# Graph attention kernel: rows sorted in interleaved groups of 512, with one-hot matmuls in place of list and output scatters

## The reference

```python
# layer 0
scores = where(adj != 0, -arange(N), -inf); vals, idx = top_k(scores, 25)
agg = max over k of x[idx[k]]            # 0 joins the maximum where degree <= 25
x = layernorm(x + relu(concat([x, agg]) @ W0 + b0))
# layer 1
Wh = x @ W1; e = leaky(s1[i] + s2[j] + emb[adj]); alpha = softmax(where(adj, e, -1e9))
x = layernorm(x + elu(layernorm(alpha @ Wh) * gamma + beta))
```

## Time and profile before

| what | us |
|---|---|
| median of 3 runs | 3402.12 (3399.23 to 3404.91) |
| span of the profiled execution, first to last instruction | 3411.3 |
| POOL busy | 2503.8 (73%) |
| DVE busy | 2400.8 (70%) |
| PE busy | 1642.6 (48%) |
| ACT busy | 1115.1 (33%) |

### The profile page before, as it was taken

How to read it: one execution, slowest core, us unless ns; L and a number is a source line. 1 busy time by engine, 2 the same in 40 slices (tenths; PEclk the granted TensorE clock), 3 DMA queues, 4 the chain that set the end, 5 groups by cost and what they waited for, 6 DMA issues and landing times.

```text
span 3411.3 us, 25793 instructions
## 1 busy us (share of the span) xinstructions
PE 1642.6 (48%) x5249; PEld 1185.4 (35%) x5259; DVE 2400.8 (70%) x5775; ACT 1115.1 (33%) x2307; POOL 2503.8 (73%) x2619
## 2 busy tenths in 40 slices
PE   8046456443463435643555345544555434466454
PEld 1034334332342323432333233333433323344343
DVE  7798877567775677767695778767785465566666
ACT  3124343323333234332343334232232212223234
POOL 3576777777677776777777777777777777777775
PEclk9976667666666666666677666676676666677776
DMA  7667876655566556675666666555544444444332
GB/s 259 211 202 258 287 240 198 226 171 183 187 197 227 171 184 198 199 246 162 216 216 194 214 195 215 163 182 153 165 131 115 123 113 116 118 118 117 106 106 72
DMA packets 221587, 610.02 MB, mean 179 GB/s; under 512 B 68849, under 2 KB 112882, under 8 KB 194802
## 3 DMA queue, kind: packets, MB, share of 16 engines
q0 software_dynamic: 122880, 342.62, 33.8%
q1 hardware_dynamic: 98546, 265.71, 22.6%
HBM read 555.19 MB, written 52.95 MB: 178 GB/s over the span
## 4 chain that ended last, share of the span: by engine, by line
POOL 63%; issue 21%; DVE 9%; DMA 3%; DVEq 2%; PE 1%; ACT 1%; SPq 0%; POOLq 0%; ACTq 0%
POOL ring L618 54%; POOL out_dram L644 3%; POOL sorted_d L595 3%; DVE agg L1206 2%; DVEq L1028 2%; DVE cand L1067 2%; POOL table_d L637 1%; POOL pair_s L628 1%; DMA adj_i<-in_adj_dram 1%; PE att_p L921 1%; DVE cand L1083 1%; DMA ring<-sorted_d,idx_cur 1%; DMA table_d<-tab,idx_loc 0%; DVE agg L1196 0%; DVE adj_h L1063 0%
## 5 line engine op out<-in xcount | busy, mean ns | idle before, releaser
L618 POOL DMA_INDIRECT ring<-table_d,idx_loc x1096 | 1051.3, 959 | 354.1 <-issue 332.9
L618 POOL DMA_INDIRECT ring<-sorted_d,idx_cur x685 | 659.4, 963 | 208.8 <-issue 208.5
L893 PE MATMUL score_p<-ident,x1k 128*128 128x128 f32 x256 | 81.2, 418 | 1429.0 <-ACT x_t L721 1425.4
L921 PE MATMUL att_p<-ring,ident 128*128 128x256 f32 (+1 forms) x2384 | 605.8, 413 | 147.3 <-DVE ring L1363 146.6
L1206 DVE TENSOR_REDUCE agg<-ring 128x256 f32<-128x2560 f32 (+9 forms) x120 | 453.6, 3780 | 254.1 <-DMA ring<-sorted_d,idx_cur 184.8
L921 PEld LDWEIGHTS att_p<-ring,ident 128*128 128x128 f32 (+1 forms) x2384 | 499.9, 211 | 251.1 <-DVE ring L1363 135.7
L893 PEld LDWEIGHTS score_p<-ident,x1k 128*128 128x128 f32 x256 | 35.8, 197 | 1478.2 <-issue 1473.7
L752 ACT ACTIVATE neg<-z 128x256 f32<-128x256 f32 x128 | 53.3, 416 | 1471.9 <-DVE z L1249 1471.9
L618 POOL DMA_INDIRECT ring<-in_x_dram,idx_cur x411 | 395.2, 961 | 132.9 <-issue 124.4
L885 PE MATMUL lin_p<-w_s,h_t 128*128 128x256 f32 x1024 | 466.8, 635 | 0.0
L885 PEld LDWEIGHTS lin_p<-w_s,h_t 128*128 128x128 f32 x1024 | 316.5, 324 | 147.6 <-issue 80.6
(11 more groups left out here) (192 smaller groups left out, 2870.3 us busy)
## 6 DMA issues: line engine op xcount, KB each, us to landing
adj_i<-in_adj_dram SPq DMA_DIRECT2D x208, 1024.0 KB, 5.4
ring<-table_d,idx_loc POOLq DMA_INDIRECT x1096, 2.8
pay<-in_x_dram SPq DMA_DIRECT2D x8, 2048.0 KB, 9.6
xs<-sorted_d SPq DMA_DIRECT2D x128, 128.0 KB, 5.9
ring<-sorted_d,idx_cur POOLq DMA_INDIRECT x685, 2.8
table_d<-tab SPq DMA_DIRECT2D x80, 132.0 KB, 4.3
ring<-in_x_dram,idx_cur POOLq DMA_INDIRECT x411, 3.6
sorted_d<-pay,rank_i POOLq DMA_INDIRECT x128, 2.5
```

Of the source, the lines that this page charges most:

```text
L618: pool.indirect_dma_start(out=to[:, k * width:(k + 1) * width], out_offset=None, in_=source, in_offset=bass.IndirectOffsetOnAxis(ap=idx_at ...
L921: last = pe.matmul(att_p[:, 0:C], ident[0:on, :], r3[0:on, s, 0:C], start=(s == 0), stop=(s == k - 1))
```

## The change

Rows are no longer sorted over the whole graph but inside groups of GROUP = 4 tiles (512 rows), and the four groups of a graph are interleaved: row s of group g becomes row 4s + g of the sorted graph. SLOTS stays as it is. A tile of the sorted group is made on TensorE: DVE writes a one-hot matrix (`pick_rows`, 128x512 float32), PE multiplies four of its 128x128 blocks with the four source tiles (`permute`, 288 columns in, 256 out), ACT copies the result (`copy_perm`) and SP stores it with a plain DMA. Layer 1's results go back the same way for graphs 0 to 6: SP stores a finished tile to `fin_d` and loads four tiles for a group (`load_fin`), and DVE, PE, ACT and SP permute and store. Only the last graph still uses `scatter_out`. This makes 128 permutes in and 112 out, at most two in a round (`order_perms`). Each is placed: "in" from four searches after its group begins, "out" from round 47 on.

The sort is done 32 times on 128 columns instead of 8 times on 512. `index_rows` on DVE (and a new wait for `idx_ld` there) replaces `list_words`, the loads of `top_cur` and `pair_cur`, and most of `check_graph`'s copies. AHEAD becomes T + 7 (23 searches before round 0), the ring has 61 slots, score banks are shared out anew, `heads` and ACT's `turn_x1` and `table` move earlier in their rounds, and `rank_rows` moves behind the next round's `max_tile`. `attend` waits for `x1t_ready`, since x1_p now shares its bank.

```diff
-AHEAD = T + 6
-RING = 63
+AHEAD = T + 7
+RING = 61
+def in_step(k):
+    g, m = k // GROUP, k % GROUP
+    if g == GROUP - 1:
+        return T
+    return GROUP * g + GROUP + m // 2
+def order_perms():
...
+    for n in range(AHEAD + ROUNDS):
+        start = len(order)
+        order += ins.get(n, [])
+        r = n - AHEAD
+        while r >= 0 and len(order) < start + 2 and outs and out_ready(outs[0][1] // T) <= r:
+            order.append(outs.pop(0))
...
 # sync
-            def load_idx(g):
-                sp.wait_ge(list_out, 16 * T * (g + 1))
...
+            def store_perm(x):
+                kind, k = PERMS[x]
+                sp.wait_ge(perm_copied, x + 1)
+                if kind == "in":
+                    b, g, m = k // T, k // GROUP % GROUP, k % GROUP
+                    rows = sorted_d[b].rearrange("(m p g) c -> g m p c", p=P, g=GROUP)
+                    sp.dma_start(rows[g, m], srt[k % 2][:, :]).then_inc(srt_out[k % 2], 16)
+                else:
+                    sp.dma_start(out_rows[k * P:(k + 1) * P, :], turned_out[k % 2][:, :]).then_inc(out_st[k % 2], 16)
+            def load_fin(k):
+                b, g = k // GROUP, k % GROUP
+                for q in range(4):
+                    sp.wait_ge(final_out[q], 16 * (T // 4) * (b + 1))
+                if k:
+                    sp.wait_ge(permuted, PERM_AT["out", GROUP * k - 1] + 1)
+                sp.dma_start(fin[:, :].rearrange("p (m c) -> p m c", c=C),
+                             fin_d[b].rearrange("(m p g) c -> g p m c", p=P, g=GROUP)[g]).then_inc(fin_ld, 16)
+            def load_idx(b):
+                for q in range(2):
+                    sp.wait_ge(srt_out[q], 16 * (T // 2) * (b + 1))
+                need(sp, idx_ready, b)
+                sp.dma_start(idx_raw[:, :].rearrange("p (u k) -> p u k", k=WORDS),
+                             sorted_d[b][:, C:SENT].rearrange("(u p) k -> p u k", p=P)).then_inc(idx_ld, 16)
 # gpsimd
-            scatter_lists(0)
             for r in range(ROUNDS + 1):
-                if first(j - LAG1):
+                if first(j - LAG1) and (j - LAG1) // T == B - 1:
                     scatter_out(j - LAG1)
-                if u == 0 and 1 <= g < B:
-                    scatter_lists(g)
 # scalar
+            def copy_perm(x):
+                kind, k = PERMS[x]
+                act.wait_ge(permuted, x + 1)
+                if kind == "in":
+                    need(act, srt_out[k % 2], 16 * (k // 2))
+                    act.activation(own_in[:, k:k + 1], perm_p[:, OWN:OWN + 1], ACT.Copy)
+                    act.activation(srt[k % 2][:, :], perm_p[:, 0:SENT], ACT.Copy).then_inc(perm_copied, 1)
...
 # tensor
+            def permute(x):
+                kind, k = PERMS[x]
+                pe.wait_ge(pick_ready, x + 1)
+                need(pe, perm_copied, x)
+                if kind == "in":
+                    g = k // GROUP
+                    pe.wait_ge(pay_ld[g % 2], 16 * (g // 2 + 1))
+                    for t in range(GROUP):
+                        last = pe.matmul(perm_p[:, 0:SENT], pick[x % 2][:, P * t:P * (t + 1)],
+                                         pay3[:, GROUP * (g % 2) + t, :], start=(t == 0), stop=(t == GROUP - 1))
...
+                    if perms[1:]:
+                        permute(perms[1])
...
 # vector
+            def pick_rows(x):
+                kind, k = PERMS[x]
+                need(dve, permuted, x - 1)
+                there = pick[x % 2][:, :].rearrange("p (t c) -> p t c", c=P)
...
+                v.tensor_tensor(there, mine.unsqueeze(2).broadcast_to([P, GROUP, P]),
+                                count[:, P * part:P * (part + 1)].unsqueeze(1).broadcast_to([P, GROUP, P]),
+                                ALU.is_equal).then_inc(pick_ready, 1)
...
+                if r and ranked_in(r - 1) is not None:
+                    rank_rows(ranked_in(r - 1))
+                if (r + IDX_LEAD) % T == 0 and 1 <= b < B:
+                    index_rows(b)
```

More of the change, by code:

```diff
@@ L52 @@
 LATER = T + 7
-AHEAD = T + 6
+AHEAD = T + 7
+IDX_LEAD = 4
 LAG0 = 9
@@ L273, in build @@
         cols_h = x1k[:, 0:N // 2]
+        count_i = ring[:, 4 * N:4 * N + GN].bitcast(I32)
+        pay3 = pay[:, :].rearrange("p (t k) -> p t k", k=SENT)
         g_heat = ring[:, 0:N]
@@ L355, in build @@
         final_out = [sem(f"final_out{q}") for q in range(4)]
+        last_out = [sem(f"last_out{q}") for q in range(4)]
         flag_put = sem("flag_put")
@@ L502, in _ @@
                     store_table(r - 6)
+                j = r - 1 - LATER - 4
+                if first(j) and j // T < B - 1:
+                    store_final(j)
                 for k in CASTS_OF[r]:
@@ L758, in roots @@
                 act.activation(std[:, :], var[:, :], ACT.Sqrt).then_inc(std_ready, 1)
-            for n in range(T):
-                cast(n)
-            totals(0)
-            for n in range(T, AHEAD + 2):
-                cast(n)
+            cast(0)
+            cast(1)
+            for n in range(AHEAD):
+                if n % GROUP == GROUP - 1:
+                    totals(n // GROUP)
+                for x in PERMS_OF_STEP[n]:
+                    copy_perm(x)
+                cast(n + 2)
             for r in range(ROUNDS - 1):
                 j = r - LATER
+                perms = list(PERMS_OF[r])
                 if first(j - 2):
+                    if first(r - 4):
+                        act.wait_ge(x1_turned, r - 3)
                     copy_att(j - 2)
+                if first(r - 4):
+                    turn_x1(r - 4)
                 if first(j - 3):
@@ L787, in _ @@
                         cast(k)
-                if first(r - 5):
-                    table(r - 5)
             def body(b):
@@ L846, in totals @@
[L846 to L855 removed]
+                    pe.matmul(score(n, c), ones_h[0:64, :], parts_h[:, at], start=False, stop=True)\
+                        .then_inc(score_ready, 1)
@@ L949, in _ @@
                         linear(r - 1)
+                    if first(r - 4):
+                        heads(r - 4)
+                    if perms[1:]:
+                        permute(perms[1])
                 else:
@@ L1084, in search_first @@
-                last.then_inc(score_used, 1)
+                for c in range(4):
+                    dve.wait_ge(score_ready, 4 * n + c + 1)
+                    v.max(cand[:, 16 * c:16 * c + 8], score(n, c)[:, 0:CH])
+                    v.max(cand[:, 16 * c + 8:16 * c + 16], score(n, c)[:, CH:2 * CH]).then_inc(score_used, 1)
+                free_pay(n)
                 settle()
-                top_lists(cand[:, :], lambda r: lists[:, n * WORDS + 8 * r:n * WORDS + 8 * r + 8], WIDEST // 8)
+                top_lists(cand[:, :], lambda c: best(n, c), WIDEST // 8)
@@ L1317, in steps @@
                     settle()
-                if sorted_in(r) is not None:
-                    degree_codes(sorted_in(r))
-                if first(n) and t == T - 1:
-                    list_words(n // T)
+                if ranked_in(r) is not None:
+                    degree_codes(ranked_in(r))
                 if first(i2):
```

512 lines of the change are left out of this document (292 added, 220 removed).

## The result

The change makes the kernel faster: 3255.85 us (4 runs, 3249.44 to 3259.41) against 3400.68 us for the kernel before beside it, a ratio of 0.9572 with a 95% interval of 0.9557 to 0.9588. Forecast were 3207 us, 0.943, and a range of 3140 to 3315. The direction was right and the gain was 145 us where 195 were forecast.

A forecast was written before the change was run, and what follows sets the result against it. POOL's indirect DMAs were taken to bound the kernel from the first layer-1 gather on, DVE before it. The span was 3411.3 + 61 - 271 + 15 = 3216, the median 9.2 under it: 3207 us, range 3140 to 3315.

The forecast's parts named there:

- POOL sets the time behind the meeting point, and what comes off it counts in full: After the first layer-1 gather, POOL never rests; list and output scatters removed there save their full price, together 271 us.
- the meeting point: POOL's first layer-1 gather, which needs all 16 tables of graph 0; forecast to move 61 us later, to about 531.
- The allowance of 15 us for rounds in which DVE is late: Behind the first layer-1 gather, uneven rounds make DVE late at times: 15 us added, bounds 0 and 80.
- the ring rival: PE and ACT wait on each other in a round, up to 30.2 us, and the kernel slows to 3558 us; chance 0.07.
- DVE's round: DVE's own time per paired round, 19.8 us before, grows by 2.3 to 22.1, staying 0.7 under POOL's 22.8.
- the rival that DVE becomes the bound: In the paired rounds DVE's addition is 4.0 us, its round 23.8, over POOL's: +80, so 3290 us; chance 0.15.
- PE, ACT and SP at nothing: In the paired rounds, permutes (2.0 or 4.3 us each), copies, stores and loads are covered and add no time.
- The clock: PE's granted clock, 0.68 before, rises with more activity, so added matmuls pay for part of themselves; the sum unchanged.
- The picks hold POOL up: Two-input picks on DVE block POOL's DMAs behind the first layer-1 gather, giving 145 us back: 3352 us; chance 0.05.

The follow-up runs named there:

- the one-input edit: Changed kernel with each pick as four 128-column compares against a scalar column, not one two-input compare: 4050.02 us, 0.9902; on a second chip 4063.6 us, 0.9927.
- the unedited kernel: The changed kernel with no further edit, timed beside the kernel before on one of the four other chips: 4057.21 us, 0.9911.

## Why the prediction was right, point by point

**POOL sets the time behind the meeting point, and what comes off it counts in full.** Mostly right. 271 us came off, 210.5 were gained, and the sum had 271 - 15 = 256. The allowance of 15 us for rounds in which DVE is late is the mis-sized term: 61 went missing. It also had another cause than the one given, for POOL waits 1.5 us in all for DVE's `agg` there. The profile shows where the 61 are. The gathers and `pair_s` DMAs that both kernels have behind the meeting point got longer by 29 us in all (from `sorted_d` 18, from `table_d` 9, `pair_s` 2). Waits for `att_p` are 39.9 us, where they were 7.6, which is 32 more. For the first, the picks' hold is a cause that the one-input edit shows, on other chips. The second is PE and ACT arriving late in single rounds, the mechanism of the ring rival at a small size: ahead of three of the four longest of these waits PE itself waited 2.4 to 3.2 us for ACT's `x_t`, the wait that the change gave `attend`. No run tests this. That on the first chip each saved us of POOL's time is a gained us wasn't tested there either; on the other chips it isn't so.

**The meeting point.** Right in sum, 529.0 against about 531. Its two parts were off in opposite ways. The first gather is at 146.98 and not 138, and DVE's first `max_tile`, forecast at 177.5, starts 11 us after that. From `max_tile` to the meeting point it took 340 us against 313 before, so +27 where I had +41, although the waits for ranks alone are 33.5 us: the instructions added on DVE hid partly in gaps. That 31 and 27 add to nearly the forecast's 20 and 41 is luck.

**DVE's round.** 2569.6 us busy against 2590 forecast. A pick measures 680 ns against 0.69. The paired rounds with a search are 82, one fewer than before since the search runs one round further ahead. They take 1898.2 / 82 = 23.1 us against POOL's forecast of 22.8. DVE's waits in this stretch for rows gathered by POOL are twelve lines from 46.2 down to 0.3, which add to 131 us, forecast under 150. Without them its round is (1898.2 - 131) / 82 = 21.6 us, against 22.1. The margin under POOL held, and the rival that DVE becomes the bound stayed away.

**PE, ACT and SP at nothing.** Right for the permutes' rate: 2.44 us on average, near the lower of the bounds 2.0 and 4.3. Not right that nothing of it shows: POOL's 32 us of added waits for `att_p` are the part of PE's and ACT's work that wasn't covered, and the sum had it at nothing. On DVE the ranks behind the permute, and `idx_raw` behind SP's other loads, make 101 us of waits. Of these 60 lie behind the meeting point, where DVE's own round stayed under POOL's. The other 41 lie ahead of it, where DVE sets the time and they should count; no run on the first chip tests it.

**The clock.** PE's granted clock behind the meeting point rose from 0.68 to 0.80. The linear matmuls fell from 635 to 580 ns each and the bias ones from 691 to 569, while `attend`'s went from 413 to 438; why is open. PE's busy time rose by 439.8 us for 551.1 us of permutes (311.8 + 239.3), so 111 came back elsewhere. In the paired rounds PE is busy 1260.7 / 82 = 15.4 us a round. The rule of the Trainium skill cited in the prediction ("TensorE: Matmul & The Clock Gate", Part 1) is that activity releases the full rate. By it things should go that way, and this trace agrees.

**The picks hold POOL up** had 5% and 145 us. It exists at a much smaller size: 43 us by the overlap (205 x 0.212), and 24 by POOL's busy time. The 240 DMAs removed were worth 112 x 1.029 + 128 x 0.963 = 238.5 us of that by the earlier trace rows, and it fell by only 214.0. What makes the difference between the two wasn't tested; two-input work that the change removed may have had holds of its own. The clearest case on the timeline of POOL and DVE:

```profile
2630.93 0.95 POOL L706 DMA_INDIRECT ring<-table_d,idx  x1 [0.30 <-issue]
...
2632.18 2.52 POOL L706 DMA_INDIRECT ring<-sorted_d,idx  x1 [0.31 <-issue]
2632.23 0.44 DVE L1399 SCALAR_TENSOR_TENSOR z<-att_s,mv,gam 128x256 f32<-128x256 f32 x1
2632.60 1.27 DVE L1267 TENSOR_TENSOR pick<-own_in,count 128x512 f32<-128x512 f32 x2
...
2635.01 0.95 POOL L706 DMA_INDIRECT ring<-sorted_d,idx  x1 [0.30 <-issue]
```

The DMA takes 2.52 us in place of 0.95, about the 1.7 us that the two-input work beside it takes. The Trainium skill ("SBUF — State Buffer", SBUF: two separate sides) has a DVE operation with two SBUF inputs and a GpSimd operation that reads SBUF exclude each other for a whole instruction. The trace agrees for some DMAs and not for others: the mean of those that overlap grows by 0.21 us and not by up to 0.68. That only a part of a DMA's preparation is held would fit, but it wasn't tested.

## What to carry to other kernels

When an engine that issues one DMA after another sets the time, count the DMAs a change removes at their full price, but allow for what the work put in their place does to the rest: here 61 of 271 us, a fifth to a quarter of the price, came back as longer DMAs and as waits for an engine that had nearly always been ahead. Look for the instruction that stands last in another engine's program order behind the added work. A gain measured on one chip should be tried on a second before the next small edit is judged by it.

## What the runs showed of the hardware

The kernel before took 3400.68 us on one chip and 4075 to 4094 on four others, with POOL's DMAs equally long (959 and 956 ns). What is added there is "issue" idle time on DVE, PE and ACT (1131.8, 1191.7 and 773.8 us in the kernel before, 11.6, 0.9 and 0.7 on the first chip), mostly at the same instructions in each run, and waits whose releaser the profile can't name. The gain of 4.3% is 0.9% there. The likely reason is that POOL no longer sets the time: in the unedited kernel on such a chip it waits 453.8 us for `att_p`, and its share of the chain is 1%.

A two-input DVE operation on 512 columns of float32 held a POOL DMA that overlapped it up by 0.21 us on average on the first chip and 0.19 in the same kernel on another, and in the longest case, beside two of them and a smaller one, by 1.57; four operations with one tensor input and a scalar column, 0.28 us each, held it by 0.015 to 0.017.
